# Softmax maxima in three key pieces with a third score bank, smaller routing steps, shared weights split early, another tail order

## What is computed

```python
# x: (2, 1024, 256), ctx: (2, 77, 256); 16 heads of 64
lat = layernorm(layernorm(x)); c = layernorm(ctx)
q = lat @ Wq
k, v = split(concat([c, lat], 1) @ Wkv)          # 1101 keys for each batch
x = x + softmax(q k^T / 8) v @ Wout
# xf: the 2048 normalised tokens; 32 experts in 8 groups, hidden size 512
shared = (silu(xf @ sg) * (xf @ su)) @ sd
# routing: 4 best groups by score, then the 4 best experts of them, gates by softmax,
# position in the expert by a running count, 320 slots for each expert
routed[tok] += gate * ((silu(buf_e @ wg_e) * (buf_e @ wu_e)) @ wd_e)
out = x + shared + routed
```

## Time and profile before

| | us |
|---|---|
| median of three runs | 1699.55 |
| profiled execution | 1705.26 |
| span of the profile | 1703.5 |
| before the first score of block 0 | 51.9 |
| the 32 blocks, 51.86 to 1162.12 | 1110.3 |
| tail, 1162.12 to 1272.60 | 110.5 |
| experts and end, 1272.60 to 1703.5 | 430.9 |

### The profile page before, as it was taken

The page is one execution under the profiler, slowest core; times in us unless marked ns, Lnnn a source line. Parts: engine busy times, 40 slices in busy tenths (PEclk is TensorE's granted clock), DMA queues, the critical chain, the costliest instruction groups (busy, mean ns, idle before and its releaser), DMA issues.

```text
span 1703.5 us, 23797 instructions
## 1 busy us (share of the span) xinstructions
PE 1545.7 (91%) x8086; PEld 1075.3 (63%) x8086; DVE 1050.0 (62%) x1576; ACT 795.4 (47%) x1499; POOL 939.5 (55%) x749
## 2 busy tenths in 40 slices
PE   3899999999999989799999889996889999999995
...
GB/s 99 12 77 81 105 77 14 10 14 10 23 14 10 23 14 10 14 10 24 29 37 24 10 14 20 34 17 81 75 90 175 177 193 167 185 178 169 193 168 93
DMA packets 99282, 117.93 MB, mean 69 GB/s; under 512 B 10595, under 2 KB 78181, under 8 KB 99173
## 3 DMA queue, kind: packets, MB, share of 16 engines
...
...
## 4 chain that ended last, share of the span: by engine, by line
PE 76%; DVE 14%; ACT 5%; issue 2%; POOL 2%; DMA 1%; SPq 0%; ACTq 0%; DVEq 0%; POOLq 0%
PE ps_o L830 14%; PE ps_t L690 9%; PE ps_m L792 8%; PE ps_m L690 8%; PE ps_st L690 8%; PE ps_st L815 7%; PE ps_st L819 6%; DVE arena_r L1185 3%; PE ps_t L850 3%; ACT arena L1443 3%; PE ps_m L727 3%; PE ps_o L727 2%; PE ps_t L895 2%; DVE arena_r L1174 1%; PE ps_t L798 1%
## 5 line engine op out<-in xcount | busy, mean ns | idle before, releaser
L635 POOL TENSOR_TENSOR arena<-arena 128x512 f32<-128x512 f32 (+1 forms) x512 | 660.8, 1292 | 387.6 <-ACT arena L1443 351.3
L1443 ACT ACTIVATE arena<-ps_st 128x512 f32<-128x512 f32 (+1 forms) x576 | 327.8, 596 | 497.5 <-PE ps_st L819 453.3
L1185 DVE TENSOR_REDUCE arena_r<-ps_m 128x1 fp32r<-128x1101 f32 x256 | 332.6, 1299 | 214.8 <-PE ps_m L792 210.3
L665 POOL DMA_INDIRECT acc_rows<-arena,ids x96 | 150.7, 1570 | 292.3 <-ACT arena L1504 264.6
L815 PE MATMUL ps_st<-arena_r 128*128 128x512 f32 (+1 forms) x576 | 267.0, 464 | 27.2 <-ACT arena L1443 27.1
L830 PE MATMUL ps_o<-arena 128*64 128x512 f32 (+1 forms) x1152 | 269.9, 603 | 0.0
L819 PE MATMUL ps_st<-arena_r 68*128 68x512 f32 (+2 forms) x576 | 234.7, 407 | 16.3 <-DVE arena_r L1192 16.3
L792 PE MATMUL ps_m<-arena_r 128*128 128x512 f32 (+1 forms) x768 | 196.9, 366 | 28.9 <-DVE arena_r L1185 24.1
L792 PEld LDWEIGHTS ps_m<-arena_r 128*128 128x128 f32 x768 | 138.0, 196 | 125.3 <-DVE arena_r L1185 56.0
L815 PEld LDWEIGHTS ps_st<-arena_r 128*128 128x128 f32 (+1 forms) x576 | 108.8, 189 | 114.4 <-ACT arena L1443 84.0
L690 PE MATMUL ps_m<-arena_r 128*128 128x320 f32 (+1 forms) x864 | 166.7, 329 | 1.3 <-DVE arena_r L1307 1.2
...
## 6 DMA issues: line engine op xcount, KB each, us to landing
...
```

What stands on the lines that cost most here:

```text
L635: pool.tensor_tensor(total, probsT[0:rows, h, 0, :] if kt == 1 else total, probsT[0:rows, h, kt, :], ALU.add).then_inc(added, 1)
L665: pool.indirect_dma_start(out=dst[:, :], in_=y_sb[par][:, c, 0:w], in_offset=None, compute_op=ALU.add, out_offset=bass.IndirectOffsetOnAxi ...
L1185: dve.tensor_reduce(neg[h][:, c:c + 1], scores_m[:, 0:KEYS], AX.X, ALU.max, negate=True)\
L1443: act.activation(probsT[0:rows, h, kt, :], ps_st[0:rows, n % 2, :], ACT.Exp).then_inc(exp_done, 1)
```

## The change

- A `max` becomes smaller: the 1101 keys are taken in three pieces of 369 columns (they overlap by a few), and a step holds two pieces, one in each of two banks, so that a block and head has six steps of two matmuls (370 columns) and one VectorE reduction over 2 x 369 in place of four steps of three matmuls and 1101. A last small reduction, `neg`, makes the four negated maxima out of twelve. `row` waits for `neg`.
- The bank that this frees goes to the scores: `ps_st` has three, and an `st` waits for the exponential three scores back. The six steps of head 1 lie in the slots (0, 0) to (0, 4) and (0, 6), those of the next block's head 0 in (0, 8) and (1, 2) to (1, 6).
- The extra events are cut into parts and put at named places: `a` in slot (1, 3) after the `av` and before the `max`, `b` before `row` in slot (1, 6), `c` at the end of (0, 5), `d` at the end of (1, 8), `ring` and `ring_early` for what TensorE does. Group 1's tokens are normalised from block 19 on, in place of block 25. `h_row` and `hT` have their own places for each group.
- Gate and up weights of the shared expert are loaded in blocks 30 and 31 into `shared_raw` (over values that are done with), and split by ScalarE (`ws`) and VectorE (`wl`) there; the down weights are still split in the tail.
- In the tail `up` events are cut into `up`, `silu`, `high`, `hid` and `lowh`, the first follows the last values at once, and the routing of groups 2 and 3 lies between them.

```diff
-        own_max = [own("max", d, 1, i) for i in range(4)]
-        next_max = [nxt("max", n, 0, i) for i in range(4)]
+        own_max = [own("max", d, 1, i) for i in range(MAX_STEPS)] + [own("neg", d, 1)]
+        next_max = [nxt("max", n, 0, i) for i in range(MAX_STEPS)] + [nxt("neg", n, 0)]
         out = [old("out", prev, i) for i in range(2)]
-        after = {(0, 8): [own("row", d, 1), old("sum", prev)],
+        after = {(0, 1): own_max[1:2],
+                 (0, 4): own_max[4:5],
+                 (0, 6): own_max[5:],
+                 (0, 8): [own("row", d, 1), next_max[0], old("sum", prev)],
                  (1, 1): [],
-                 (1, 2): [old("norm", prev), next_max[0]],
-                 (1, 3): first_values + [next_max[1]]}
+                 (1, 2): [old("norm", prev), next_max[1]],
+                 (1, 3): first_values + [next_max[2]],
+                 (1, 4): [out[0], next_max[3]]}
         if project:
-            after[0, 0] = [own_max[0]] + project_k(0) + [own_max[1], k_low[0]]
+            after[0, 0] = [own_max[0]] + project_k(0)
+            after[0, 1] += [k_low[0]]
             after[0, 2] = project_k(2) + [own_max[2], k_low[2]]
-            after[0, 3] = project_k(1) + [k_low[1]]
-            after[0, 5] = project_q() + [q_again] + last_values + [q_low, own_max[3]]
-            after[1, 4] = [out[0], next_max[2]]
-            after[1, 5] = [nxt("v", pp, 0), next_max[3]]
-            after[1, 6] = more_values + [nxt("row", n, 0), out[1]]
+            after[0, 3] = project_k(1) + [own_max[3], k_low[1]]
+            after[0, 5] = project_q() + [q_again] + last_values + [q_low]
+            after[1, 5] = [nxt("v", pp, 0), next_max[4]]
+            after[1, 6] = next_max[5:] + more_values + [nxt("row", n, 0), out[1]]
             after[1, 7] = [nxt("v", pp, 1)]
             after[1, 8] = [nxt("v", pp, 2)]
         else:
-            after[0, 0] = [own_max[0]] + project_q() + [own_max[1]]
-            after[0, 3] = [own_max[2]]
-            after[0, 5] = [q_again] + last_values + [q_low, own_max[3]]
-            after[1, 4] = [out[0], next_max[2]]
-            after[1, 6] = [out[1], next_max[3]] + more_values + [nxt("row", n, 0)]
+            after[0, 0] = [own_max[0]] + project_q()
+            after[0, 2] = [own_max[2]]
+            after[0, 3] = [own_max[3]]
+            after[0, 5] = [q_again] + last_values + [q_low]
+            after[1, 5] = [next_max[4]]
+            after[1, 6] = next_max[5:] + [out[1]] + more_values + [nxt("row", n, 0)]
...
+    def put(block, h, kt, place, *events):
+        extra.setdefault((block // QUADS, block % QUADS, h, kt), []).extend((place, ev) for ev in events)
+    def a(block, *events):
+        put(block, 1, 3, "mid", *events)
+    def b(block, *events):
+        put(block, 1, 6, "row", *events)
+    def c(block, *events):
+        put(block, 0, 5, "end", *events)
+    def d(block, *events):
+        put(block, 1, 8, "end", *events)
+    def ring(block, *events):
+        put(block, 1, 0, "end", *events)
+    def ring_early(block, *events):
+        put(block, 0, 2, "end", *events)
+    for j in range(FILLS):
+        put(1 + j, 0, 6, "end", ("fill", j))
+    a(0, ("cenn",))
+    for i in range(4):
+        a(6 + 2 * i, ("zs", i))
+        ring(7 + 2 * i, ("zt", i))
+        a(7 + 2 * i, ("ze", i))
+        d(7 + 2 * i, ("zl", i))
+    a(16, ("stat_a", 0))
+    b(16, ("stat_b", 0))
+    a(17, ("stat_a", 1))
+    b(17, ("stat_b", 1))
+    put(17, 1, 7, "end", ("root", 0), ("root", 1))
+    a(18, ("norm_a", 0))
+    b(18, ("norm_b", 0))
+    d(18, ("norm_c", 0))
+    ring(19, ("turned", 0, 0))
+    a(19, ("low", 0, 0))
+    b(19, ("norm_a", 1))
+    d(19, ("norm_b", 1))
+    ring_early(20, ("turned", 0, 1))
+    c(20, ("low", 0, 1))
+    ring(20, ("score", 0))
+    a(20, ("scored", 0), ("top", 0))
+    b(20, ("mask_a", 0))
+    d(20, ("mask_b", 0))
+    a(21, ("best_a", 0))
+    b(21, ("best_b", 0))
+    d(21, ("norm_c", 1))
+    put(22, 0, 4, "end", ("gexp", 0))
+    c(22, ("hot_a", 0))
+    a(22, ("hot_b", 0))
+    b(22, ("hot_c", 0))
+    d(22, ("gates", 0))
+    ring(23, ("pos", 0))
+    a(23, ("places_a", 0))
+    b(23, ("places_b", 0))
+    ring_early(24, ("turned", 1, 0))
+    c(24, ("low", 1, 0))
+    ring(24, ("turned", 1, 1))
+    a(24, ("low", 1, 1))
+    ring(25, ("score", 1))
+    a(25, ("scored", 1), ("top", 1))
+    b(25, ("mask_a", 1))
+    d(25, ("mask_b", 1))
+    c(26, ("best_a", 1))
+    a(26, ("best_b", 1), ("hot_a", 1))
+    b(26, ("hot_b", 1))
+    d(26, ("hot_c", 1))
+    put(26, 1, 4, "end", ("gexp", 1))
+    ring(27, ("pos", 1))
+    a(27, ("places_a", 1))
+    b(27, ("gates", 1))
+    d(27, ("places_b", 1))
+        put(24 + i // 4, *spots[i % 4], "end", ("scat", 0, i))
+        put(28 + i // 4, *spots[i % 4], "end", ("scat", 1, i))
+    put(30, 0, 6, "end", ("wload", 0))
+    put(30, 1, 7, "end", ("ws", 0))
+    c(31, ("wl", 0))
+    put(31, 0, 6, "end", ("wload", 1))
+    put(31, 1, 5, "end", ("ws", 1))
+    put(31, 1, 6, "end", ("wl", 1), ("wload", 2))
+    put(31, 1, 7, "end", ("stat_a", 2), ("stat_b", 2))
+    put(31, 1, 8, "end", ("root", 2))
...
-    tail = end[:3] + [("normed", 2), end[3], ("turned", 2, 0), ("turned", 2, 1), ("low", 2, 0), ("low", 2, 1),
-                      end[4], ("ws", 2), ("score", 2), end[5], end[6], ("stat", 3), ("root", 3)]
-    tail += ups(0, 0, 1) + [("top", 2), ("mask", 2), ("normed", 3), ("turned", 3, 0), ("turned", 3, 1),
-                            ("low", 3, 0), ("low", 3, 1), ("best", 2), ("hot", 2), ("gexp", 2)]
-    tail += ups(0, 2, 3) + [("score", 3), ("pos", 2), ("gates", 2), ("places", 2)] + scats[2]
-    tail += [("low_hid", 0), ("down", 0), ("top", 3), ("mask", 3), ("best", 3), ("hot", 3), ("gexp", 3), ("accout", 0)]
-    tail += ups(1, 0, 1) + [("pos", 3), ("gates", 3), ("places", 3)] + scats[3] + ups(1, 2, 3)
-    tail += [("low_hid", 1), ("down", 1), ("accout", 1)]
-    tail += ups(2, 0, 1, 2, 3) + [("low_hid", 2), ("down", 2), ("accout", 2)]
-    tail += ups(3, 0) + [("ws1", 0)] + ups(3, 1) + [("ws1", 1)] + ups(3, 2) + [("ws1", 2)] + ups(3, 3)
-    tail += [("low_hid", 3), ("down", 3), ("accout", 3)]
+    av, total, norm, outs = end[:3], end[3], end[4], end[5:]
+
+    def hidden(c, ht):
+        return [("up", c, ht), ("silu", c, ht)] + ([("high", c, ht - 1)] if ht else []) + \
+               [("hid", c, ht)] + ([("lowh", c, ht - 1)] if ht else [])
+
+    def last(c):
+        return [("high", c, HIDS - 1), ("lowh", c, HIDS - 1), ("down", c), ("accout", c)]
+
+    tail = av + [("up", 0, 0), ("norm_a", 2), ("norm_b", 2), total, ("silu", 0, 0), ("up", 0, 1), ("turned", 2, 0),
+                 ("turned", 2, 1), ("hid", 0, 0), norm, ("silu", 0, 1), ("low", 2, 0), ("low", 2, 1), ("hid", 0, 1),
+                 ("ws", 2), ("wl", 2), ("norm_c", 2), ("up", 0, 2), ("score", 2), ("scored", 2)] + outs
+    tail += [("silu", 0, 2), ("high", 0, 0), ("lowh", 0, 0), ("hid", 0, 2), ("stat_a", 3), ("stat_b", 3), ("root", 3),
+             ("high", 0, 1), ("lowh", 0, 1), ("top", 2), ("up", 0, 3), ("mask_a", 2), ("mask_b", 2), ("silu", 0, 3),
+             ("hid", 0, 3), ("high", 0, 2), ("lowh", 0, 2), ("norm_a", 3), ("norm_b", 3), ("best_a", 2), ("best_b", 2),
+             ("turned", 3, 0), ("turned", 3, 1), ("high", 0, 3), ("lowh", 0, 3), ("hot_a", 2), ("hot_b", 2),
+             ("hot_c", 2), ("gexp", 2), ("low", 3, 0), ("low", 3, 1), ("norm_c", 3), ("pos", 2), ("score", 3),
+             ("gates", 2), ("places_a", 2), ("places_b", 2), ("scored", 3)] + scats[2]
+    tail += [("down", 0), ("accout", 0)] + hidden(1, 0) + [("top", 3), ("mask_a", 3), ("mask_b", 3)] + hidden(1, 1)
+    tail += [("best_a", 3), ("best_b", 3), ("gexp", 3), ("hot_a", 3)] + hidden(1, 2) + [("hot_b", 3), ("hot_c", 3)]
+    tail += hidden(1, 3) + [("pos", 3), ("gates", 3), ("places_a", 3), ("places_b", 3)] + scats[3] + last(1)
+    tail += hidden(2, 0) + hidden(2, 1) + hidden(2, 2) + hidden(2, 3) + last(2)
+    for ht in range(HIDS):
+        tail += hidden(3, ht) + ([("ws1", ht)] if ht < WPIECES else [])
+    tail += last(3)
...
+    PIECE = -(-(KEYS - 1) // KEY_PIECES) // 2 * 2
+    PIECE_W = KEYS - (KEY_PIECES - 1) * PIECE
...
-        ps_m = stack.enter_context(nc.psum_tensor("ps_m", [P, 3, 512], F32))
-        ps_st = stack.enter_context(nc.psum_tensor("ps_st", [P, 2, 512], F32))
+        ps_m = stack.enter_context(nc.psum_tensor("ps_m", [P, 2, 512], F32))
+        ps_st = stack.enter_context(nc.psum_tensor("ps_st", [P, 3, 512], F32))
         ps_o = stack.enter_context(nc.psum_tensor("ps_o", [P, 512], F32))
         ps_t = [stack.enter_context(nc.psum_tensor(f"ps_t{i}", [P, 512], F32)) for i in range(2)]
-        scores_m = ps_m[:, :, :].rearrange("p a n -> p (a n)")
-        ey_bank = (ps_o, ps_m[:, 2, :])
+        ey_bank = (ps_o, ps_st[:, 2, :])
         z_bank = [[ps_st[:, 0, :], ps_st[:, 1, :]], [ps_m[:, 0, :], ps_m[:, 1, :]]]
-        zc_bank = ps_m[:, 2, :].rearrange("p (k n) -> p k n", k=DT)
```

(35 more changed lines are left out.)

212 lines of the change are left out of this document (107 added, 105 removed).

## The result

The changed kernel takes 1708.59 us (median of 8 runs, 1705.64 to 1714.55), the one before 1700.47 beside it (8 runs). The ratio is 1.0051, with a 95% interval of 1.0034 to 1.0068. The forecast was 1672 with a range up to 1704: wrong in sign, and outside the range.

The account below looks back on a forecast made before the run. TensorE, busy in 91% of the span, was taken as the bound, so gains must come from its waits or work. Terms 23 - 33 - 3 - 3 + 1 - 12 = -27 us on 1699.6 gave 1672 us, range 1640 to 1704.

Parts of the forecast that it names:

- Smaller maxima: Clean blocks: a pair gets 1.5 us slower with the third bank counted in, +23 us over 15.5 pairs.
- the ledger: Gains and losses of a clean pair added up, -3.3 - 1.3 - 1.5 + 7.2 = +1.1 us.
- slot by slot: A clean pair laid out with the same durations: even block 30.9 us, odd block 36.4, +2.0 a pair.
- The third bank: Scores in clean blocks: a third bank removes all waits for exponentials, 3.3 us a pair.
- Routing in small steps: Blocks with routing: 7.5 us a group in place of 24, -33 us (bounds -40 and -18).
- Rival 2: Small steps still come late: routing saves the 18 of its bound, the tail nothing; 1699 us, chance 0.15.
- `zs`: Four `zs` steps that cost 1.8 us each, one 3.4: two operations at `a` stick out by 1.5; -3 us.
- Block 31: The last block loses its adjacent pair of maxima and its slow clock but gets the tight steps: -3 us.
- Start: The start of the kernel has six steps of maxima in place of four: +1 us.
- Tail: After the last block: first `down` after some 35 us, not 42.6, second chunk gains 4; -12 us (bounds -22 and 0).
- rival 3: Clock falls in the tight stretches of even blocks: 1698 us, or 1724 with a second fall a pair; chance 0.12.
- the cycle's bounds: Nine tight places a pair: a cycle of maxima from 1.4 to 1.7 us gives +9 to +37 us.

Follow-up runs that it names:

- e7: e2 with the scores in two of their three banks, the third idle: 1675.6 us, a clean pair 66.8 us.
- e9: The changed kernel with the scores in two of their three banks, the third idle: 1729.2 us, a clean pair 69.4 us.
- e4: The changed kernel with the routing of groups 0 and 1 back in lumps at the old places: 1747.4 us (one run).
- e1: The changed kernel with whole maxima, two score banks and the old slots again; small routing steps, early split and new tail stay: 1667.3 us.
- e2: The changed kernel with each piece of the maxima a step of its own, the two banks used in turn: 1665.1 us.
- e6: e2 with a third tail order, the first `down` ahead of group 3's transposes and remaining routing spread over later chunks: 1659.1 us.
- e8: e1 with the tail order of e6: 1660.0 us.

## Why the prediction was wrong

**Smaller maxima, +23 forecast, +48 measured.** This is the step that failed: the term was made of +1.5 us a pair, and a pair measured +3.0. Its cycle was right (1.52 to 1.62 forecast, 1.51 to 1.63 measured), and so were the reduction (0.92 both), most of the places, and the full clock. What was too small is the sum of the waits in a pair. Half a microsecond of it was my own choice between the two sums, +1.1 by the ledger and +2.0 slot by slot; the latter was the better one, and I took the middle. Slot by slot the even block was to take 30.9 us and took 31.7, the odd one 36.4 and took 36.6, so most of the other 1.0 lies in the even block. In blocks 2 and 3 of the changed kernel the starts of TensorE's groups give about 8.3 us of delay where the ledger had 7.2. What follows a maximum that waited comes 0.10 us later than behind one that didn't (0.44 instead of 0.34 us, nine times), and the wait for `row` is 0.45 in one block and 0.58 in the other. A wait of some 0.4 us before the first `out` of the even block was not in the list at all. The profile puts it down to "issue", but the program waits there for GpSimd's `norm`, and in block 4 `norm` ends at 214.22:

```profile
212.94 1.28 POOL L730 TENSOR_TENSOR arena<-arena 128x512 f32<-128x512 f32 x1
```
```profile
214.33 1.10 PE L941 MATMUL ps_t<-wout_sb,arena 128*128 128x256 f32 x4 [0.38 <-issue]
```

The prediction had put at nothing what the waits do to ScalarE and GpSimd ("both have slack"); there is no wait before this `out` in the timeline of block 4 before the change. With 8.3 the ledger says +2.2; the last 0.8 I can't place. A small error a pair, taken 16 times, is most of 25 us.

**The third bank, -3.3 a pair.** The waits did go, as forecast (27.1 to 0.7 us idle). But that is not what the bank is worth: alone, in the new order, it gives 1.1 to 1.2 us a pair (e7, e9). The pieces that make room for it cost, with their slots, 4.1 us a pair when two banks are filled together (69.4 against 65.3) and 1.5 in turn (66.8), so bank and pieces together lose 3.0 in the one form and 0.3 in the other.

**Routing in small steps, -33.** Right. It is 37.5 us (e4) or 34.4 (e1). Rival 2 fell for these blocks.

**`zs`, -3.** Right. Against four clean pairs of the same kernel, blocks 6 to 13 took 11.4 us more before and 6.9 more in the changed kernel, 4.4 less, of which 3.8 are in the even blocks, where the `zs` steps lie. In e1, with the old slots, those blocks went from 272.6 to 270.1, and there the even ones gained nothing (125.6 before, 125.8 in e1).

**Block 31, -3:** 34.49 to 31.74 us, right. That e1 with the old slots stays at 34.40 fits the cause that was given. The faster kernels don't have this gain, though: in e2 the block takes 34.2 us, with a wait of 4.3 us for GpSimd's `norm` and a fall of the clock. **Start, +1:** +2.3; block 0's six steps meet the cycle too.

**Tail, -12 forecast, 0 measured.** The wait of 6 to 9 us before group 3's transposes was named, and it was 9.3. What was missed is the second one behind it, 6.1 us before `pos`: VectorE's queue goes on with `best`, the low half of a hidden tile that waits 2.2 us for ScalarE, `hot` and group 3's `low`, and `pos` and the scores stand behind that on TensorE. So the first `down` came 39.1 us after the last values and not 35, and group 3's `pos` in the next chunk waited 4.8 us, where it had waited 2.5. Then the clock was at 1.2 GHz from 1184.8 to 1208.7 us and for another 10.2 us from 1225.7, 34 us in the tail against 24 before; the second `down` took 9.9 us in place of 7.2. VectorE is busy for 29.3 of the 39.2 us, so an order that puts its work ahead of the first `down` can only move the wait; e6 and e8 gained since they put it behind.

**The sum.** The two errors, 25 and 12 us, less some 7 us that routing, `zs` and the first blocks came out better, explain the distance between -27 and the +3 of the profiles. Of the rivals none was this one: rival 3 gave 1698 to 1724 us on the slower side, but through the clock, and the clock in clean blocks was at 1.00. The range was too narrow because the cycle's bounds covered its length (1.4 to 1.7, +9 to +37), not the count and the surroundings of its places; 48 is outside even those. The bounds were also too narrow by the prediction's own rule: at 14 us for 0.1 us of cycle, 1.4 to 1.7 us is a width of 42 us, and +9 to +37 has 28.

## What to carry over

When an engine fills banks that another must empty before the next fill, smaller pieces shorten each turn but don't overlap the two. With the two banks given to alternate pieces, the same pieces took 43 us less here. Price a recurring wait by laying out the whole block once, slot by slot, with every engine that a wait holds up. Believe that sum rather than a ledger of gains and losses, and multiply its error by the number of repeats before giving a range. And in the stretch of the tail where VectorE had more to do than TensorE, a new order paid only once VectorE's work moved behind the next large piece of TensorE's.

## What the runs showed of the chip

Waits of 0.55 us, three in a row, and two more of 0.8 and 0.55 us in each even block left the clock at 1.00: blocks 2 to 11 of the changed kernel. With the additional waits of 0.3 to 0.4 us for exponentials in e9 it fell five times in the stretch from 200 to 640 us, each time in an even block, for 3.4 or 6.8 us. That bears on the rule of the Trainium skill weighed in the prediction ("TensorE: Matmul & The Clock Gate", section "A second HAM failure mode: psum-queue depth-cycling"): the clock did not go up and down in blocks 2 to 11 of the changed kernel, and in e9 it did at times. What decides is open. Blocks 2 and 4 of e9 show the same waits within 0.03 us, and only block 4 had a fall. These are single profiled executions, and no run varied the waits alone.

A reduction of 369 elements a partition out of PSUM took 533 ns, 738 took 920 and 1101 took 1299: by these three some 1.05 ns an element and 0.15 us for the instruction. Twice as many of half the length cost VectorE 25 us of busy time in e2, which the overlap paid back.
